# Turning the quantised FFN rows by a transposing DMA instead of on TensorE: a fused cross-attention and FFN layer

## The reference

```python
x = x + xattn(layernorm(x), ctx_1024, ctx_1024, proj_q, bias_q, proj_k, bias_k, proj_v, bias_v, w_out)
x = x + ffn(layernorm(x), w_gate, w_up, w_down)      # ffn:
xq = fp4_quant_dequant(x)          # blocks of 16 along the last axis
gate, y = xq @ fp4(w_gate).T, xq @ fp4(w_up).T       # 256 -> 704
h = silu(gate) * y
out = fp4_quant_dequant(h) @ fp4(w_down).T           # 704 -> 256
```

## Time and profile before

| | us |
|---|---|
| runs of the kernel before | 392.68, 393.39, 396.76 (median 393.39) |
| the profiled execution, its own time | 393.67 |
| span of its instructions in the trace | 391.6 |
| mean granted TensorE clock in it, as a share of full | 0.969 |

### The profile page before, as it was taken

The page is one execution under the profiler, slowest core; times in us unless marked ns, Lnnn a source line. Parts: engine busy times, 40 slices in busy tenths (PEclk is TensorE's granted clock), DMA queues, the critical chain, the costliest instruction groups (busy, mean ns, idle before and its releaser), DMA issues.

```text
span 391.6 us, 9504 instructions
## 1 busy us (share of the span) xinstructions
PE 333.4 (85%) x3571; PEld 254.3 (65%) x3571; DVE 307.2 (78%) x629; ACT 263.7 (67%) x634; POOL 259.0 (66%) x272
## 2 busy tenths in 40 slices
PE   1778759998799898989987978888779999999976
PEld 1455447776588686868765756676556767767854
DVE  1979844756767888777788876689999999998792
ACT  3666687996889999999986979734443453542431
POOL 7272244786579898997995886647844668767510
PEclk9989958999999999999998999999998999999999
DMA  7990535769559899899994896911000000000001
GB/s 215 321 359 4 103 67 103 124 120 170 103 104 180 168 152 182 169 184 170 175 186 95 135 163 134 148 31 28 13 14 15 13 26 17 14 15 28 16 27 40
DMA packets 131710, 42.42 MB, mean 108 GB/s; under 512 B 123788, under 2 KB 129616, under 8 KB 131665
## 3 DMA queue, kind: packets, MB, share of 16 engines
q1 hardware_dynamic: 131665, 41.82, 54.7%
HBM read 8.78 MB, written 2.10 MB: 28 GB/s over the span
## 4 chain that ended last, share of the span: by engine, by line
DVE 37%; PE 27%; POOL 16%; ACT 10%; issue 8%; DMA 2%; SPq 0%; ACTq 0%; DVEq 0%
POOL arena L1396 8%; PE ps L501 5%; PE ps L503 4%; PE ps L502 4%; DVE arena L1200 4%; ACT arena L861 4%; DVE arena L1202 3%; PE ps L580 3%; DVE arena L1150 3%; POOL arena L1401 3%; DVE arena L1323 3%; DVE negmax L1119 3%; PE ps L637 3%; DVE arena L1289 2%; POOL wffn L1426 2%
## 5 line engine op out<-in xcount | busy, mean ns | idle before, releaser
L1396 POOL TENSOR_TENSOR arena<-arena 128x640 f16<-128x640 f32 x64 | 93.7, 1465 | 57.3 <-ACT arena L871 57.3
L861 ACT ACTIVATE arena<-ps,negmax 128x154 f32<-128x154 f32 x256 | 79.1, 407 | 12.2 <-DVE negmax L1119 12.0
L1119 DVE TENSOR_REDUCE negmax<-ps 128x4 f32<-128x616 f32 x64 | 50.9, 795 | 18.3 <-PE ps L637 18.0
L580 PE MATMUL ps<-v_h,pT 128*128 128x132 f16 (+1 forms) x640 | 52.5, 213 | 11.5 <-DVE q_odd L1111 5.4
L580 PEld LDWEIGHTS ps<-v_h,pT 128*128 128x128 f16 x640 | 38.9, 99 | 18.0 <-issue 16.2
L1401 POOL TENSOR_TENSOR arena<-arena 128x256 f16<-128x256 f32 x64 | 44.6, 698 | 8.0 <-ACT arena L878 8.0
L871 ACT ACTIVATE arena<-arena 128x640 f16<-128x640 f32 x64 | 48.0, 750 | 1.1
L501 PE MATMUL ps<-arena 128*128 128x256 f16 (+1 forms) x144 | 41.5, 288 | 7.4 <-DVE arena L1022 6.0
L501 PE MATMUL ps<-arena,xnT_even 128*128 128x352 f16 x128 | 40.1, 313 | 4.9 <-DVE xnT_even L1211 4.2
L502 PE MATMUL ps<-arena 128*128 128x256 f16 (+1 forms) x144 | 41.3, 287 | 0.0
L503 PE MATMUL ps<-arena 128*128 128x256 f16 (+1 forms) x144 | 41.2, 286 | 0.0
(11 more groups left out here) (164 smaller groups left out, 943.3 us busy)
## 6 DMA issues: line engine op xcount, KB each, us to landing
out_dram<-arena SPq DMA_DIRECT2D x16, 128.0 KB, 1.7
pT<-arena SPq DMA_TRANSPOSE x70, 4.1
xs<-in_x_dram SPq DMA_DIRECT2D x2, 512.0 KB, 7.3
arena<-in_L_xattn_w_out_dram SPq DMA_DIRECT2D x1, 1024.0 KB, 11.8
xs<-in_x_dram SPq DMA_DIRECT2D x2, 384.0 KB, 6.7
wffn<-in_L_ffn_w_down_dram SPq DMA_DIRECT2D x1, 704.0 KB, 9.5
wffn<-in_L_ffn_w_gate_dram SPq DMA_DIRECT2D x1, 640.0 KB, 7.6
wffn<-in_L_ffn_w_up_dram SPq DMA_DIRECT2D x1, 640.0 KB, 8.5
```

Source lines behind the costliest of these rows:

```text
L580: last = pe.matmul(o[:, h0 * HB:h1 * HB], pT[:, n % RING_P, part * CHUNKS + c], v[:, b, j, at[0]:at[-1] + 1].rearrange("p m k -> p (m k)") ...
L861: last = act.activation(prob[:, j, k * LP:k * LP + L], ps[:, 2 * (j % 2) + k % 2, (k // 2) * L:(k // 2 + 1) * L], ACT.Exp, bias=negmax[:, ...
L1119: dve.tensor_reduce(negmax[:, s, 4 * j:4 * j + 4].rearrange("p (k u) -> p u k", k=2), v, AX.X, ALU.max, negate=True).then_inc(max_done, 1)
L1396: pool.tensor_tensor(part_of(j, 1), prob[:, j], part_of(j, 0), ALU.subtract).then_inc(p_low, 1)
```

## The change

From step 1 on, `xq` is split in SBUF and turned by DMA. ACT copies both tiles' rows as f16 high part into `xqsplit[:, i % 2]`, a new view with two buffers in `q_odd`, the queries of the odd steps, which are no longer read in the FFN; POOL subtracts the low part; SP issues one transposing DMA of the 128x1024 f16 buffer into `rows_turned(i)`, that is `xnT_odd` for odd steps and `xnT_even` for even ones. `turn_xq` on PE, `xq_high` out of PSUM on ACT and `xq_low` on DVE are taken out. The sign moves into the scales of the silu and of `hidden`.

```diff
+        xqsplit = q_odd.rearrange("p h a t -> p (h a t)")[:, 0:8 * D].rearrange("p (k s a n) -> p k s a n", k=2, s=2, a=2)
 SP
+            def turn_xq(i):
+                sp.wait_ge(xq_lo, i)
+                if i == 1:
+                    sp.wait_ge(task_mm, TASK_AT[query_tasks(STEPS - 1)[-1]] + 1)
+                else:
+                    sp.wait_ge(gu_mm, 2 * i - 2)
+                sp.dma_start_transpose(rows_turned(i).rearrange("p s a c n -> p (s a c) n"),
+                                       xqsplit[:, i % 2].rearrange("p s a n -> p (s a n)")).then_inc(xq_turned, 16)
             for n in range(SLOTS + HID_LAG):
                 turn(n)
+                if n - HID_LAG == TAIL[0][1][1]: turn_xq(1)
...
+            turn_xq(2)
             for i in range(STEPS):
+                if i + 3 < STEPS: turn_xq(i + 3)
                 store(i)
 PE
-            def turn_xq(i, s):
...
             def gate_up(i, s):
-                if t >= 2: pe.wait_ge(xqt_low, t - 1)
+                if t >= 2: pe.wait_ge(xq_turned, 16 * i)
...
-                        last = three(ps[:, m, 0:GU], xnT_even[:, s, 0, c], xnT_even[:, s, 1, c],
+                        last = three(ps[:, m, 0:GU], v[:, s, 0, c], v[:, s, 1, c],
 ACT
-            def xq_high(i, s):
-                act.wait_ge(xqt_mm, 2 * i + s - 1)
-                act.activation(xnT_even[:, s, 0].rearrange("p c t -> p (c t)"), ps[:, XT_BANK, 0:D], ACT.Copy,
-                               scale=-1.0).then_inc(xqt_high, 1)
+            def xq_high(i):
+                act.wait_ge(xq_done, i + 1)
+                wait(act, xq_turned, 16 * (i - 2))
+                act.activation(xqsplit[:, i % 2, :, 0], xq, ACT.Copy).then_inc(xq_hi, 1)
...
-                    if not (peeled(i, 0) and s == 0) and exists(shift(i, s, 1)[0]): xq_high(*shift(i, s, 1))
+                    if s == 0 and exists(i + 1): xq_high(i + 1)
 DVE
-            def xq_low(i, s):
-                dve.wait_ge(xqt_high, 2 * i + s - 1)
-                dve.scalar_tensor_tensor(l, ps[:, XT_BANK, 0:D], -1.0, h, ALU.mult, ALU.subtract).then_inc(xqt_low, 1)
...
                     hidden(i, s)
-                    if not (peeled(i, 0) and s == 0) and exists(shift(i, s, 1)[0]): xq_low(*shift(i, s, 1))
 POOL
             def round_x(i):
-                wait(pool, xqt_mm, 2 * i - 2)
...
+            def xq_low(i):
+                pool.wait_ge(xq_hi, i)
+                pool.tensor_tensor(xqsplit[:, i % 2, :, 1], xq, xqsplit[:, i % 2, :, 0], ALU.subtract).then_inc(xq_lo, 1)
...
                     if s == 1 and exists(i + 2): value_x(i + 2)
+                    if s == 0 and exists(i + 1): xq_low(i + 1)
                     if not last_tile(i, s): value_h(i, s)
```

More of the change, by code:

```diff
@@ L253, in xattn_ffn_kernel @@
         xmagic, xsummed, xgrid, xq_done = sem("xmagic"), sem("xsummed"), sem("xgrid"), sem("xq_done")
-        xqt_mm, xqt_high, xqt_low = sem("xqt_mm"), sem("xqt_high"), sem("xqt_low")
+        xq_hi, xq_lo, xq_turned = sem("xq_hi"), sem("xq_lo"), sem("xq_turned")
         gu_mm, silu_done, hid_ready = sem("gu_mm"), sem("silu_done"), sem("hid_ready")
@@ L690, in _ @@
                 if n >= PROJ_LAG: project(n - PROJ_LAG)
-            def turn_xq(i, s):
[L693 to L699, removed]
             def gate_up(i, s):
                 t = 2 * i + s
-                if t >= 2: pe.wait_ge(xqt_low, t - 1)
+                v = rows_turned(i)
+                if t >= 2: pe.wait_ge(xq_turned, 16 * i)
                 if t == 0:
@@ L746, in ffn @@
                     gate_up(i, s)
-                    if not (peeled(i, 0) and s == 0) and exists(shift(i, s, 1)[0]): turn_xq(*shift(i, s, 1))
                     for t in tail_of(2 * i + s):
@@ L848, in high @@
                     act.activation(xnT_even[:, :, 0].rearrange("p s c n -> p s (c n)"),
-                                   task_out(t).rearrange("p (s n) -> p s n", s=B), ACT.Copy, scale=-1.0).then_inc(task_high, 1)
+                                   task_out(t).rearrange("p (s n) -> p s n", s=B), ACT.Copy).then_inc(task_high, 1)
                 else: o_high(t)
@@ L962, in silu_gate @@
                 act.activation(silu.rearrange("p (m n) -> p m n", m=2), ps[:, 0:2, 0:GU], ACT.Silu,
-                               scale=1.0 / FS).then_inc(silu_done, 1)
+                               scale=-1.0 / FS).then_inc(silu_done, 1)
             def h_high(i, s):
@@ L1185, in low @@
                     h, l = (xnT_even[:, :, part].rearrange("p s c n -> p s (c n)") for part in range(2))
-                    dve.scalar_tensor_tensor(l, task_out(t).rearrange("p (s n) -> p s n", s=B), -1.0, h,
-                                             ALU.mult, ALU.subtract).then_inc(task_low, 1)
+                    dve.tensor_tensor(l, task_out(t).rearrange("p (s n) -> p s n", s=B), h, ALU.subtract).then_inc(task_low, 1)
                 else: o_low(t)
@@ L1206, in grid_x @@
                 minus_grid(x_tmp, xsummed, xgrid, i)
-            def xq_low(i, s):
-                dve.wait_ge(xqt_high, 2 * i + s - 1)
-                h, l = (xnT_even[:, s, part].rearrange("p c t -> p (c t)") for part in range(2))
-                dve.scalar_tensor_tensor(l, ps[:, XT_BANK, 0:D], -1.0, h, ALU.mult, ALU.subtract).then_inc(xqt_low, 1)
             def minus_grid_w(w, half):
@@ L1288, in hidden @@
                 dve.wait_ge(silu_done, t + 1)
-                dve.scalar_tensor_tensor(hid[:, s].rearrange("p (m n) -> p m n", m=2), ps[:, 2:4, 0:GU], 1.0 / FS,
+                dve.scalar_tensor_tensor(hid[:, s].rearrange("p (m n) -> p m n", m=2), ps[:, 2:4, 0:GU], -1.0 / FS,
                                          silu.rearrange("p (m n) -> p m n", m=2), ALU.mult, ALU.mult).then_inc(hid_ready, 1)
```

## The result

The changed kernel takes 395.91 us (median of 20 runs), the kernel before 394.32 us (20 runs beside them): ratio 1.0052, 95% interval 1.0029 to 1.0074. By that ratio it is slower by about 2.1 us (1.1 to 2.9), where 395.7 us and +2.33 had been forecast, and this lies within the one per cent that was called no change.

What follows compares the result with a forecast made beforehand. The prediction took DVE's list, waits included, to bound FFN steps up to tile 11, then PE. Its terms summed to +2.33 us on 393.67, 396.0 profiled, less 0.28: 395.7 us, with 8 in 10 for 393.3 to 398.0.

Steps and rivals of the forecast that it cites:

- tile 2: FFN tile 2: ACT's `xq_high(2)` delays the last turned weights' copy and POOL's subtraction holds DVE, +1.31 us.
- tile 4: FFN tile 4: priced like a steady tile with s = 0, +0.43 us from POOL's hold on DVE.
- tiles 12 and 13: Late FFN: tile 12's hold delays `h_low`, on which `down` and PE's last tiles hang, +0.43 us.
- The bound: FFN steps: DVE's list sets the 15.10 us step up to tile 11; only tiles 13 to 15 are PE's.
- The gap behind `hidden`: DVE between `hidden` and `scales_h`: removing `xq_low` of 0.41 us gives back only 0.14 us a tile.
- POOL's subtraction: POOL in tiles with s = 0: new 128x512 `xq_low` takes 1.15 us and holds a DVE instruction, +0.43 us.
- ACT's wait for `round_x`: ACT in tiles with s = 0: idle 2.4 us ahead of `xq_high`, delaying the magnitude; +0.10 us on DVE alone.
- The DMA: Transposing DMA each step: issued 323.2, landed by 328.2, next step's `gate_up` at 336.4, so 8 us of cover.
- rival D: DMA landing becomes the wait: 0.6 us in tile 4 at worst, every s = 0 tile if over 12 us; no separate chance.
- Rival A: FFN: POOL's subtraction doesn't hold DVE and the wait is hidden; +0.27 us, 393.7 us; chance 0.14.
- Rival C: FFN: removed DVE work comes back whole, 0.33 us a tile in 13 tiles; 389.1 us; chance 0.05.
- Rival B: FFN: POOL costs more than one hold, through longer holds and a later `round_h`; 396.8 to 398.3 us; chance 0.17.

Runs made afterwards that it cites:

- e5: Kernel before the change, with DVE's `xq_low` on 8 columns instead of 256; step 14.84 us (before 15.10), first to last `hidden` 117.16 us (before 118.86).
- e3: Changed kernel with POOL's subtraction on 4 columns a tile instead of 256, ACT's wait kept; step 15.03 us, first to last `hidden` 118.66 us.
- e4: Changed kernel with ACT's `magnitude_h` ahead of `xq_high` and POOL's subtraction on 4 columns a tile; step 14.84 us, first to last `hidden` 116.78 us.
- e1: Changed kernel with ACT's `magnitude_h` ahead of `xq_high`; step 15.40 us, ratio to the kernel before 1.0051.
- e2: Changed kernel with ACT copying the last turned weights ahead of `xq_high(2)` in tile 2 only; tile 2 7.80 us (changed kernel 8.34), step 15.40 us.
- e6: Changed kernel with the transposing DMA of steps 3 to 7 held some 5 us longer; step 17.58 us, 404.21 us in one run.
- e8: Changed kernel with `magnitude_h` ahead of `xq_high` and POOL's whole subtraction behind `value_h`; step 14.94 us, first to last `hidden` 122.32 us.
- e11: Changed kernel with `magnitude_h` ahead of `xq_high` and POOL's whole subtraction done twice; step 15.57 us, first to last `hidden` 123.82 us.
- e7: Changed kernel, magnitude first, POOL's subtraction split into halves around `value_h`, two transposing DMAs a step; 392.41 us, ratio 0.9954 to the kernel before.
- e9: The split-subtraction kernel (e7) with the second half moved behind `round_h`; step 14.91 us, ratio to the kernel before 0.9992.

## Why the prediction was right, point by point

The terms of the sum against the two profiles; a tile is measured from its `hidden` to the next one.

| term | predicted | measured |
|---|---|---|
| tile 1 | -0.33 | -0.33 |
| tile 2 | +1.31 | +1.20 |
| tile 3 | 0 | -0.01 |
| tile 4 | +0.43 | +0.60 |
| tiles 6, 8, 10, each | +0.43 | +0.43, +0.42, +0.43 |
| tiles 5, 7, 9, 11, each | -0.14 | -0.13 |
| tiles 12 and 13 | +0.43 | -0.26 + 0.68 = +0.42 |
| tile 14 | -0.24 | -0.22 |
| sum | +2.33 | +2.42 |

- The bound: DVE's list sets the step up to tile 11. Right, and shown: PE got 0.5 us of busy time back a step and the step grew. e5, which takes work from DVE alone, shortens it.
- The gap behind `hidden`: a removed 0.41 us is worth 0.14. Right; e5 measured 0.13.
- POOL's subtraction: 1.15 us taken from the line through two sizes, 1.16 measured. That it holds L1205 is shown by e3 against the changed kernel and by e4 against e1, pairs that differ in its length alone; the second pair gives its price without the wait. L1205 took 1.27 us, a little more than the 1.1 to 1.2 given as a sign. That its end fits to 0.01 us (3.85 us after the start of `hidden`, 3.86 forecast) is partly luck: POOL's subtraction ended 0.06 sooner than forecast, and L1205 0.74 after it instead of 0.69. The Trainium skill, SBUF — State Buffer, section "Who interferes with whom", has the pair of ports held for a whole instruction by whoever starts first; the trace agrees down to e2's row, where POOL started 0.02 us ahead and DVE's 0.19 us took 1.18.
- ACT's wait for `round_x`: 2.4 us of idle time forecast, 2.27 measured, +0.10 for DVE if alone. Its copy took 0.63 and not 0.67. e3 still has the wait and lasts 7.35 against 7.29 before: +0.06. One reason why it is less is that `round_x` starts 0.15 us after `hidden` starts and no longer 0.22, which the prediction didn't have; the change takes a wait on PE out of `round_x`, but no run shows that this is the reason.
- Tile 2 came out at 1.20 for 1.31. The copy of 0.63 and the earlier `round_x` make some 0.1 of it. e1 and e2 show both causes at work there, but together with the hold, not as a sum of separate prices.
- Tile 4 cost 0.17 more than a steady tile. The small instructions of the layer norm stand there on DVE, and they too take turns with POOL (L1051, of 0.10 us, takes 0.67 beside the subtraction); I had used the steady tile's price. With the subtraction cut short (e3) tile 4 falls from 9.36 to 8.62, so it was the hold. The sum came near by luck here: tile 2's 0.11 too much and tile 4's 0.17 too little nearly cancel.
- Tiles 12 and 13: the 0.43 comes one tile later than its hold, and by the forecast path. `h_low` ends 0.43 us later after `hidden(12)`, and PE's `down` waits for it, as PE's timeline shows:

```profile
357.60 0.70 PE L744 MATMUL ps<-xs,ident_y 128*128 128x256 f32 x2 [0.94 <-DVE arena L1322]
```

- The level, 395.7 forecast and 395.91 measured, is in part luck: it was worked out from 393.39 us for the kernel before, whose median in 20 runs is 394.32. The change's own part is +2.33 forecast against 2.1 by the ratio, 1.6 between the two medians, and 2.42 by the stretch.
- The DMA: the step that was wrong, without harm. The prediction put the next step's `gate_up` at 336.4 and its cover at 8 us. But 321.3 is `gate_up` of the odd tile of step i, and the one that needs the turned rows comes one tile later, at 328.5, not two. The same pair in the changed kernel, by the timelines of SP and PE:

```profile
339.63 1.25 SPq L490 DMA_TRANSPOSE xnT_even<-q_odd  x1
...
345.36 0.31 PE L516 MATMUL ps<-arena,xnT_even 128*128 128x352 f16 x1
```

Landing took 2.7 us there, less than the 3.9 of rows 8 from the busy attention: some 3 us of cover. A landing of 5.7 us, not of over 12, would have been enough to hold `gate_up` back, and e6 shows that a turn 5 us later costs 2.2 us a step; so rival D was much nearer than I wrote. With the 3.9 us of rows 8 it would still have been covered, by 1.8.
- Rival A fell by e3: a subtraction that doesn't hold DVE would have given about its stretch of 118.66, not 121.28. Rival C fell by e5: the gain is 0.13 a tile even when nothing is added. Rival B's longer holds aren't in the rows: the steady step has one new hold, of 0.44 us.

## What to carry to other kernels

Before work is moved off a full engine, look at what follows it there: if the next instruction reads the result of the one before, the removed one lay partly in a pause and gives back less than its duration (here 0.13 of 0.41 us). A VectorE list that is full should be read together with GpSimd's timeline, pair by pair, for each instruction with two operands in SBUF and for the short TENSOR_SCALAR, which was held too (e2); where in GpSimd's list a piece stands mattered about as much here (15.40 against 14.94 us a step, e1 and e8, with the same instructions) as that it was added at all (15.40 against 14.84, e1 and e4). And two causes that lie beside each other can only be told apart by taking away both, then each: e1 alone would have said that the wait on ACT is nothing, and the steady step of e11 alone that the hold is nothing.

## What the runs showed of the hardware that was not expected

- Holds between VectorE and GpSimd need not add up. Doubling the GpSimd instruction (e11) held one VectorE instruction 0.84 us longer and freed another of 0.95, net 0.17 a step, but cost 1.18 in tile 2, where none was freed. Of two kernels with the same instructions, the second half of the subtraction ahead of `round_h` or behind it (e7 against e9), one is 0.37 us a step faster.
- A transposing DMA of 128x1024 f16 took 2.7 us to landing in the FFN, where the DMA engines are nearly idle (the last of seven 4.3), and 3.2 to 5.0 us, median 3.9, in the attention; half of it took 2.4 (e7, median).
- After 2.21 us without work and some 0.8 us at full clock TensorE ran for some 3.2 us at half of it, 1.2 GHz (0.67 over 5.1 us, e6), and a wait of 2.2 us became a delay of 3.9. After 3.66 us without work it had 1.2 GHz for the next 5.7 us (e8).
